# Graph layers on one core: relational stage by single steps with tables of its own, attention weights in PSUM, shared weighing, bias on TensorE

## Time and profile before

| | |
|---|---|
| median of 3 runs | 4223.15 us (4221.75 to 4224.39) |
| the profiled execution | 4219.4 us, span 4217.6 us |
| first stages, to the first gather of attention | 178.5 us |
| attention's gathers, first to last start | 178.5 to 1375.3 us |
| `project_relations`, first to last L1740 | 2230.2 to 2598.5 us |
| relational gathers, first to last start | 2605.7 to 3706.4 us |
| PE, DVE, ACT, POOL busy, share of the span | 83%, 67%, 46%, 55% |

### The profile page before, as it was taken

The page is one execution under the profiler, slowest core; times in us unless marked ns, Lnnn a source line. Parts: engine busy times, 40 slices in busy tenths (PEclk is TensorE's granted clock), DMA queues, the critical chain, the costliest instruction groups (busy, mean ns, idle before and its releaser), DMA issues. The chain is left out here.

```text
span 4217.6 us, 67721 instructions
## 1 busy us (share of the span) xinstructions
PE 3496.7 (83%) x17983; PEld 2727.1 (65%) x17984; DVE 2818.7 (67%) x7798; ACT 1935.8 (46%) x5274; POOL 2319.3 (55%) x2470
## 2 busy tenths in 40 slices
PE   8788888888888799799989997877878777866793
PEld 4466666666666699799975444655656555645692
DVE  5499999999999655411112222888888888875456
ACT  2355555555555233233322334666666666636230
POOL 5477777777777155400002222777777777737441
PEclk9899999999999999899999998788887888765896
DMA  6677777777777411111113445555565556534446
GB/s 190 200 210 203 202 206 205 207 205 201 203 207 205 151 40 40 56 35 37 35 55 150 178 178 195 170 175 171 168 178 170 168 168 176 160 107 147 122 133 217
DMA packets 266461, 656.43 MB, mean 156 GB/s; under 512 B 52764, under 2 KB 140984, under 8 KB 250408
## 3 DMA queue, kind: packets, MB, share of 16 engines
q0 software_dynamic: 128768, 394.47, 33.2%
q1 hardware_dynamic: 130328, 251.92, 17.4%
q10 hardware_dynamic: 7056, 6.43, 0.4%
HBM read 521.34 MB, written 131.29 MB: 155 GB/s over the span
## 5 line engine op out<-in xcount | busy, mean ns | idle before, releaser
L278 POOL DMA_INDIRECT attn_KV<-kv_tab,attn_stage x880 | 930.1, 1057 | 279.6 <-issue 252.1
L1846 POOL DMA_INDIRECT rel_V<-h_tab,rel_stage x880 | 833.9, 948 | 309.0 <-issue 229.6
L1949 PE MATMUL rel_SP<-rel_V,rel_OH 128*128 128x264 f32 x1760 | 608.5, 483 | 3.6 <-DVE node L2018 1.7
L379 PE MATMUL attn_QP<-node,attn_OHT 128*128 x1760 | 507.4, 414 | 10.2 <-issue 5.5
L391 PE MATMUL attn_SP<-attn_KV 128*128 128x264 f32 x1760 | 494.7, 407 | 20.9 <-DVE node L493 20.3
L1949 PEld LDWEIGHTS rel_SP<-rel_V,rel_OH 128*128 128x128 f32 x1760 | 372.6, 233 | 75.7 <-ACT rel_OH L1884 10.5
L391 PEld LDWEIGHTS attn_SP<-attn_KV 128*128 128x128 f32 x1760 | 344.9, 201 | 94.8 <-issue 37.7
L2018 DVE TENSOR_TENSOR node<-node,rel_SP 128x264 f32 x880 | 366.0, 416 | 50.5 <-PE rel_SP L1949 28.2
L379 PEld LDWEIGHTS attn_QP<-node,attn_OHT 128*128 128x128 f32 x1760 | 334.1, 203 | 61.3 <-issue 14.6
L1740 PE MATMUL pr_H<-WX,pr_YT 128*128 128x512 f32 x784 | 345.3, 593 | 0.0
L454 DVE TENSOR_TENSOR attn_KV<-attn_KV,attn_QP 128x512 f32<-128x512 f32 x440 | 298.0, 677 | 56.0 <-DMA attn_KV<-kv_tab,attn_stage 55.9
(11 more groups left out here) (393 smaller groups left out, 6761.0 us busy)
## 6 DMA issues: line engine op xcount, KB each, us to landing
rel_OHT<-dst_rows SPq DMA_DIRECT2D x55, 1024.0 KB
h_tab<-pr_H SPq DMA_DIRECT2D x49, 1056.0 KB, 4.0
attn_KV<-kv_tab,attn_stage POOLq DMA_INDIRECT x880, 3.8
rel_V<-h_tab,rel_stage POOLq DMA_INDIRECT x880
pair_Y<-y SPq DMA_DIRECT2D x105, 130.0 KB, 2.1
kv_tab<-qkv_KV SPq DMA_DIRECT2D x49, 256.0 KB, 2.5
mix_Y<-y_out SPq DMA_DIRECT2D x49, 256.0 KB, 4.3
attn_runs<-runs SPq DMA_DIRECT2D x55, 192.0 KB
```

Of the source, the lines that this page charges most:

```text
L278: pool.indirect_dma_start(out=KV[:, i * IT + u, 0:2 * FEAT], out_offset=None, in_=d["kv_tab"][:, :], in_offset=bass.IndirectOffsetOnAxis(a ...
L379: mm = pe.matmul(QP[(2 * i + v) % BANKS][:, (u % 2) * FEAT:(u % 2 + 1) * FEAT], OHT[:, u, :], query(blks[v]), start=True, stop=True)
L1846: pool.indirect_dma_start(out=V[:, i * IT + u, :], out_offset=None, in_=d["h_tab"][:, :], in_offset=bass.IndirectOffsetOnAxis(ap=stage[:, ...
L1949: pe.matmul(SP[(c * IT + u) % SUMS][:, 0:NUMC], OH[:, j * IT + u, :], V[:, j * IT + u, :], start=True, stop=True).then_inc(s["sums"], 1)
```

## The change

In attention the weights get a bank of their own (`WB`) and VectorE reads them there; ScalarE still copies them to SBUF for the denominators. VectorE weighs seven of eight pairs (`OWN` = 7), ScalarE the last with 16 activations (`weigh_last`). The bias is added by a matmul with the identity into the scores' bank, and VectorE's `add_bias` and the tile `TB` go; scans and maxima read the scores from PSUM. `QP` has two banks instead of three. The relational stage runs over steps of single tiles, 832 in 52 groups, with one block number per step; its tables (`dst_in`, `idx_src`, `runs`, `links`, `dst_rows`, `relmask`, `block_of`) are made in `project_relations`, whose loops are written out. `project_with_tables` no longer gathers types nor makes `dst_rows`, `relmask` and `idx_rel`.

```diff
+SINGLES = -(-(TILES + LAST_BLOCK) // IT) * IT
+SINGLES_PAD = SINGLES + IT
...
     (attention_layer)
-    BANKS = 3
+    BANKS = 2
     LEAD = 3
+    OWN = PAIRS - 1
...
-        T, W = CH[:, 0:P], CH[:, P:2 * P]
+        WB = ctx.enter_context(nc.psum_tensor("attn_WB", [P, 512], F32))
+        T, W = CH[:, 0:P], WB[:, 0:P]
+        weights = W.rearrange("p (h s) -> p s h", s=IT)
...
     (ScalarE)
+                def weigh_last(c, j):
+                    if has(c, G):
+                        for u in (IT - 2, IT - 1):
+                            at = j * IT + u
+                            for h in range(HEADS):
+                                mm = act.activation(KV[:, at, FEAT + h * DH:FEAT + (h + 1) * DH],
+                                                    KV[:, at, FEAT + h * DH:FEAT + (h + 1) * DH], ACT.Identity,
+                                                    scale=KV[:, at, 2 * FEAT + h:2 * FEAT + h + 1])
+                        mm.then_inc(s["last_weighted"], 1)
...
                     masks(k + 1, 0)
+                    if has(k - 2, G):
+                        act.wait_ge(s["w_copied"], k - 1)
+                    weigh_last(k - 2, (i + 1) % 3)
                     distances(k + 1, 1)
                     move_masks(k, i, 1)
...
     (TensorE)
-                        pe.wait_ge(s["weighted"], c * PAIRS + (v + 1))
+                        if v < OWN:
+                            pe.wait_ge(s["weighted"], c * OWN + (v + 1))
+                        else:
+                            pe.wait_ge(s["last_weighted"], c + 1)
...
-                        pe.transpose(T, ST[:, :], m.ident[:, :]).then_inc(s["st_turned"], 1)
+                        pe.matmul(T, ST[:, :], m.ident[:, :], start=True, stop=False).then_inc(s["st_turned"], 1)
+                        pe.wait_ge(runs_in[j], landed(turn, j != 2) * (16 * 5))
+                        pe.matmul(T, m.ident[:, :], bias[:, j, :], start=False, stop=True).then_inc(s["biased"], 1)
...
                         pe.wait_ge(s["exp"], g + 1)
+                        need(pe, s["weighted"], g * OWN)
                         pe.transpose(W, EX[:, :], m.ident[:, :]).then_inc(s["w_turned"], 1)
...
     (VectorE)
-                    if has(c, G) and v < PAIRS:
+                    if has(c, G) and v < OWN:
...
-                        dve.tensor_tensor(rows, rows, KV[:, at:at + 2, 2 * FEAT:ROW].unsqueeze(3).to_broadcast([P, 2, HEADS, DH]),
+                        dve.tensor_tensor(rows, rows, weights[:, 2 * v:2 * v + 2, :].unsqueeze(3).to_broadcast([P, 2, HEADS, DH]),
                                           ALU.mult).then_inc(s["weighted"], 1)
...
-                        dve.tensor_tensor(TB[:, :], T, bias[:, j, :], ALU.add).then_inc(s["biased"], 1)
...
-                        dve.tensor_tensor_scan(A[:, :], runs[:, j, 0:P], TB[:, :], -BIG, ALU.add, ALU.max).then_inc(s["scan"], 1)
+                        dve.tensor_tensor_scan(A[:, :], runs[:, j, 0:P], T, -BIG, ALU.add, ALU.max).then_inc(s["scan"], 1)
...
     (project_with_tables: types, local, relmask and idx_rel go on all engines)
-                    if 21 <= t < 21 + SGROUPS:
-                        gather(raw["typ"], "typ", t - 21, "typ")
...
-                        sp.dma_start(d["relmask"][:, :], relmask[:, :]).then_inc(p["out"], 16)
...
     (project_relations, each engine)
-        f = norm_front(nc, m, ctx, "pr", BLOCKS)
+        f = norm_front(nc, m, ctx, "pr", BLOCKS, banks=1)
...
-                pipeline(sp, body, LEAD, 1, BLOCKS)
+                with nc.allow_non_contiguous_dma(reason="one column of the tiles' destinations"):
+                    sp.dma_start(last_i[:, :], d["dst"][0:TILES, P - 1:P].rearrange("t o -> o t")).then_inc(p["last"], 16)
+                for t in iterations:
+                    body(t, t % 2)
+                    tables(t)
...
     (SP's tables: where in the iterations the stores and loads stand)
+                    if t == 8:
+                        sp.wait_ge(p["jf"], 32)
+                        sp.dma_start(m.block_of[0:1, 0:SINGLES_PAD], d["ji"].rearrange("k p -> (k p)")[0:SINGLES_PAD].rearrange("(o s) -> o s", o=1)
+                                     ).then_inc(p["block_of"], 16)
...
+                    if t == 17:
+                        sp.wait_ge(p["local"], 1)
+                        sp.dma_start(d["dst_rows"][0:FULL * P, :].rearrange("(k p) n -> p k n", p=P), local[:, 0:FULL, :]).then_inc(p["out"], 16)
+                    if t == 26:
+                        sp.wait_ge(p["scaled"], 4)
+                        sp.dma_start(d["runs"][0:FULL * P, :].rearrange("(k p) n -> p k n", p=P),
+                                     runs[:, 0:FULL, :, :].rearrange("p k a b -> p k (a b)")).then_inc(p["out"], 16)
+                    if t == 41:
+                        sp.wait_ge(p["masked"], MASKS)
+                        sp.dma_start(d["relmask"][:, 0:SINGLES_PAD * RELS], relmask[:, :]).then_inc(p["out"], 16)
...
     (VectorE's tables begin)
+                    if t == -6:
+                        dve.wait_ge(p["last"], 16)
+                        dve.wait_ge(p["iota"], 2)
+                        link(dve.tensor_scalar(last_i[:, :], last_i[:, :], 7, None, ALU.arith_shift_right))
+                        dve.tensor_copy(tile_f[:, :], tile_i[:, :])
+                        link(dve.tensor_copy(last_f[:, :], last_i[:, :]))
+                        dve.tensor_tensor(last_f[:, :], last_f[:, :], tile_f[:, :], ALU.add).then_inc(p["ends"], 1)
...
     (relational_layer)
-    G = ITS
+    G = SINGLES // IT
...
-            return nc.values_load_multi_w_load_instructions(m.block_of[0:1, bass.ds(g * PAIRS, PAIRS)], engines=[engine], min_val=0,
+            return nc.values_load_multi_w_load_instructions(m.block_of[0:1, bass.ds(g * IT, IT)], engines=[engine], min_val=0,
...
-                                           m.sd[:, bass.ds(blks[u // 2] * RH, RH)], start=True, stop=True)
+                                           m.sd[:, bass.ds(blks[u] * RH, RH)], start=True, stop=True)
...
-                        acc = m.node[:, bass.ds(blks[u // 2] * NUMC, NUMC)]
+                        acc = m.node[:, bass.ds(blks[u] * NUMC, NUMC)]
```

More of the change, by code:

```diff
@@ L689, in project_with_tables @@
         s = sems(nc, m, "qkv", "w mm q_out kv_out kv_free stored0 stored1")
-        p = sems(nc, m, "prep", "last iota link ends ends_sb less bsel rows jt_turned jt jf jb dst src typ attr sent cleared "
-                 "steps ids block_of rawf turned turned_sb ne tail scaled pl links mixed masked local out")
+        p = sems(nc, m, "prep", "last iota link ends ends_sb less bsel rows jt_turned jt jf jb dst src attr sent cleared "
+                 "steps ids block_of rawf turned turned_sb ne tail scaled pl links mixed out")
         x_in = [new_sem(nc, m, f"qkv_x_in{i}") for i in range(2)]
@@ L1580, in project_relations @@
     with ExitStack() as ctx:
+        p = sems(nc, m, "one", "last iota link ends ends_sb less bsel rows jt_turned jt jf jb dst src typ sent cleared "
+                 "steps ids block_of rawf turned turned_sb ne tail scaled pl links mixed masked local out")
         s = sems(nc, m, "pr", "mm sc_mm h_out sc_out d_out stored0 stored1 rows_free "
@@ L1707, in body, with to_float @@
                                         SP_[i][:, RH:2 * RH].rearrange("p (r h) -> p h r", h=HEADS)).then_inc(s["d_out"], 1)
-                pipeline(dve, body, LEAD, 1, BLOCKS)
+                link = Link(dve, p["link"])
+                short = Link(dve, p["tail"])
+                def to_float(n, order):
+                    dve.wait_ge(p[n], 16 * SGROUPS)
+                    need(dve, p["turned"], 2 * order)
+                    dve.tensor_copy(rawf[:, :, :], raw[n][:, :, :]).then_inc(p["rawf"], 1)
@@ L1711, in _ @@
+                dve.memset(sent[0:1, 0:1], -1)
+                dve.memset(sent[0:1, 1:2], 1 << 20).then_inc(p["sent"], 1)
+                dve.memset(ids[:, FULL, :], 0).then_inc(p["cleared"], 1)
+                for t in iterations:
+                    body(t, t % 2)
+                    tables(t)
             @block.tensor
@@ L1855, in restage @@
                     if has(k, G):
-                        act.copy(stage[:, i * IT:(i + 1) * IT], m.idx_rel[:, bass.ds(k * IT, IT)]).then_inc(s["staged"], 1)
+                        act.copy(stage[:, i * IT:(i + 1) * IT], m.idx_src[:, bass.ds(k * IT, IT)]).then_inc(s["staged"], 1)
                 def near(k, q):
```

317 lines of the change are left out of this document (252 added, 65 removed).

## The result

The changed kernel takes 4094.11 us (median of 4 runs, 4091.63 to 4098.1); the kernel before took 4222.45 in the same job (4221.58 to 4224.39). The ratio is 0.9696, 95% interval 0.968 to 0.9713: 128 us faster, and the prediction was 4094.0. The profiled execution took 4098.1 us (span 4096.2).

The account below looks back on a forecast made before the run. GpSimd's gathers were taken to pace both edge stages. 4219.4 - 76 (attention) - 60 (relational) - 3 (`project_with_tables`) + 10 (`project_relations`) = 4090; the median, 3.75 us above, gives 4094 us, range 4068 to 4148.

Parts of the forecast that it names:

- The bound and the cause of the slow gathers: GpSimd paces both edge stages; in attention, weighings with two SBUF operands add 109 ns to the mean gather.
- the 2 KB rows: Rival for attention: these rows, not the weighing, make gathers slow; period stays 21.7 us, total 4166 us, chance 0.08.
- Attention, VectorE: Period: 21.0 us less 0.8 (bias 0.20, one weighing 0.60), plus 0.2 reserve, gives 20.4; stage -76 us.
- Attention, ScalarE: Sixteen added activations at 0.22 us, 3.5 us a period, fit; the exponential starts at 811.2 us.
- The factor: Attention: leaves ScalarE at 811.6 us, after the exponential began; VectorE asks at 811.76, so it just fits.
- Rival B: Attention: new wait from two banks or slower ScalarE; period 21.1 to 21.4 us, total about 4140 us, chance 0.14.
- Attention, TensorE's clock: Half-clock moments leave little room in 20.2 us; 0.2 us reserve a period, also for engines of nearly equal pace.
- Relational stage: 52 groups for 55, GpSimd alone pacing at 20.03 us a period: -60 us, bounds -60 and -34.
- The longer block-number loads: Relational stage: sixteen numbers for eight; VectorE's wait for gathered rows hides another 0.5 us a period; uncovered, 26 us.
- `project_relations`: TensorE's added work 3 us, stores 2, later fold some 5: +10 us in all, bounds +3 and +22.
- the lead-in: `project_relations`: last destinations land at 2213 us, behind 2 MB of `WN`; the head fold starts some 5 us later.
- the tables at their lower bounds: Table-making stages at their low ends, `project_with_tables` -8 and `project_relations` +3 us, used for the range's low end, 4068.

Follow-up runs that it names:

- e1: Kernel before, with only the weighing's weights read from PSUM (own bank, two banks of query rows for three): 4176.11 us, ratio 0.9885.
- e2: Changed kernel, with VectorE's seven weighings reading their weights from SBUF again: 4109.94 us, ratio 0.9721.
- e3: Changed kernel with all eight weighings on VectorE and none on ScalarE: 4119.15 us, ratio 0.9754.
- e5: Changed kernel with a second pair weighed by ScalarE, all 32 activations in a row ahead of the exponential: 4272.87 us, ratio 1.0109.
- e10: Changed kernel, VectorE in the relational stage loading its sixteen block numbers twice a period and using both sets: 4115.88 us, ratio 0.9741.
- e9: e6 with the load of the last destinations moved between the attention vectors and `WN`: 4073.7 us, ratio 0.9642.
- e6: Changed kernel with a second pair weighed by ScalarE, its activations in two halves in ScalarE's idle times: 4078.04 us, ratio 0.9646.
- e11: e9 plus idle TensorE transposes, 13 at the entry of `attend_and_route` and 41 in `project_relations`, on a slow chip: 4611.29 us, ratio 0.9976.
- e12: e9 plus only the 13 idle TensorE transposes at the entry of `attend_and_route`: 4068.9 us, ratio 0.9637.

## Why the prediction was right

*The bound and the cause of the slow gathers.* Right, and shown by e1 and e2: the operand in SBUF makes them slow, not the 2 KB rows. The excess of one gather is the rest of the weighing less some 0.13 us, and it falls mainly on those that begin in a weighing, so the mean of 109 ns can't be scaled by the number of weighings (e2).

*Attention, VectorE.* The period of 20.4 us is 20.36, but by other terms than those of the sum. From 21.02 (e1) the bias took 0.20, as predicted (21.02 to 20.81, e3), and the weighing 0.45 for 0.60. The 0.2 us that I had added for TensorE's clock and for two engines of nearly equal pace came from neither: 0.15 was missing from the weighing, 0.105 of it because the head sums stand right behind their product (e3). That the size fits is luck. The stage gained 79.7 us for 76.

*Attention, ScalarE.* From the first of the sixteen to the exponential 6.45 us were predicted, 6.19 found; an activation takes 0.21 us for 0.22. The factor fitted by 0.6 us, for 0.2. That this was a cliff and not a formality is shown by e5: 3.5 us more in that place cost 179 us. Rival B, a new wait in attention, didn't come: TensorE waits 36.7 us of 815 for products (two banks), and VectorE has no listed wait for TensorE.

*Attention, TensorE's clock.* The reserve was meant for moments at half clock. There were none: TensorE's wait ahead of the turned masks, 1.98 us in the earlier trace rows, is 0.8 at most now, and the clock stays at 2.4 GHz.

*Relational stage.* -60 predicted, -54.6 found. Three groups of 20.04 us are 60.1. Back came 0.07 us in each of 52 periods (3.6 us: the gathers are at 952 ns instead of 948) and 1.9 us behind the last gather. The longer block-number loads were covered, as predicted: 0.77 us of the wait for rows is still left. e10 shows where that cover ends. The typical gather is no slower (median 946 ns before, 947 after); those over 0.98 us have become more, 22 of 880 before and 33 of 832 after. What they meet there was not pursued.

*`project_relations`.* +10 predicted, +12.4 found, by terms: the lead-in 8.7 for 5 (the last destinations landed 12.6 us into the stage, not 9; the 2.4 us on one partition and the waiting behind them came as described, and two pairs of products of 1.67 us a pair, at half clock, came on top); behind the fold, the stage is longer by 3.6 us, which TensorE's added work fills (3 predicted; 21 transposes are 3.3 us in the page's count), so that nothing is left for the stores, put at 2.

*`attend_and_route`.* Missed. I had no term for a stage whose code doesn't change. Of the +5.0 us 3.0 are a longer time at the low clock at its entry and 1.3 a later load. Whether they belong to the change is open: e9, with the same code in this stage and the new attention before it, took 379.9 us.

The misses cancel in part. On the profiled execution the sum was -129 us and the span gave -121.4, while the medians differ by 128.3; the profiled run of the changed kernel was its slowest. That the median was met to 0.1 us is luck; that the sum was within 8 us of the span is not. One bound was added up wrong: attention at -87 with the tables at their lower bounds gives 4071 us, where the text has 4068.

## What to carry to other kernels

When VectorE and GpSimd's gathers share SBUF, look for gathers of two lengths in one group and for what VectorE runs beside the long ones; an operand moved to PSUM freed them here. Where two engines are within a few per cent of each other, moving work by load alone is a gamble: put it where the receiving engine now waits, and compare its next deadline with the chain behind it (e5 and e6 are the same load, 195 us apart). Don't count an engine's idle share as cover for an added cost: in e10 the wait for the pacing engine gave 0.7 of 1.12 us and the other waits little. And over a ring of buffers a lag shows at the end of the stage, not in the pace of its steady part.

## What the runs showed of the hardware

- A gather begun while a VectorE product with both operands in SBUF has more than 0.2 us to run ends 0.80 to 0.86 us behind that product (136 of 140 before, 89 of 90 in e2), and so takes up to 1.5 us for 0.95. With one operand in PSUM none of 138 took over 0.96 us (e1).
- On VectorE an instruction of 0.67 us is followed by an independent one after 597 ns, but by one that reads its result after 703 ns (changed kernel, head sums behind the fifth product).
- Sixteen ScalarE activations of 128x32 with a scale pointer take 3.49 us, a start every 0.21 us.
- Loading block numbers into registers on VectorE costs 0.06 us each: 0.46 us for eight, 0.98 for sixteen (39.3/40), 2.10 for thirty-two.
- TensorE's idle time between two stages costs more than itself: behind 5 to 8 us of idleness it ran at half clock for 10 to 20 us, and the entry of the stage took 2 to 5 us longer than where the clock had not fallen (e11, e12). Thirteen transposes of no use prevented it in one place; 41 in another, started after the clock had fallen, did not bring it back for the work that mattered.
- One chip ran the kernel before at 4623.55 us instead of 4225. In e11's profile on it GpSimd waits in attention for TensorE (137.0 us of 800) and for "remote" (61.1 us), while a gather itself lasts 946 ns as elsewhere. Of the gain that e9 and e12 have elsewhere (ratio 0.964) e11 kept next to nothing there (0.9976). Why that chip is slower is open:

```profile
L282 POOL DMA_INDIRECT attn_KV<-kv_tab,attn_stage x504 | 476.9, 946 | 323.8 <-PE attn_SP L414 137.0 <-issue 125.7 <-remote 61.1
```
